# Graph attention on one Trainium2 core: the sixth chunk's four place products are issued ahead of its four transposing passes

## The reference, cut to what matters

```python
def gatv2_layer(x, Ws, bs, Wd, bd, attn, src, dst):
    hs = (x @ Ws + bs).reshape(N, H, HD)
    hd = (x @ Wd + bd).reshape(N, H, HD)
    hs_e = hs[src]
    e = jax.nn.leaky_relu(hs_e + hd[dst], SLOPE)
    logits = jnp.einsum('ehd,hd->eh', e, attn)
    m = jax.ops.segment_max(logits, dst, num_segments=N)
    ex = jnp.exp(logits - m[dst])
    s = jax.ops.segment_sum(ex, dst, num_segments=N)
    alpha = ex / s[dst]
    out = jax.ops.segment_sum(alpha[..., None] * hs_e, dst, num_segments=N)
    return jax.nn.elu(out).reshape(N, DM)
```

## Time and profile before

| what | value |
|---|---|
| median of three runs | 2142.82 us |
| the profiled execution | 2140.68 us, span 2138.9 us |
| granted TensorE clock, mean | 0.986 of 2.4 GHz |
| TensorE busy | 2052.9 us, 96% |
| VectorE busy | 1641.7 us, 77% |
| ScalarE busy | 1160.9 us, 54% |
| GpSimd busy | 975.4 us, 46% |
| passes of line 601 | 4368 instructions |
| products of line 605 | 4368 instructions |

### The profile page before, as it was taken

How to read it: one execution, slowest core, us unless ns; L and a number is a source line. 1 busy time by engine, 2 the same in 40 slices (tenths; PEclk the granted TensorE clock), 3 DMA queues, 4 the chain that set the end, 5 groups by cost and what they waited for, 6 DMA issues and landing times. The chain is left out here.

```text
span 2138.9 us, 85423 instructions
## 1 busy us (share of the span) xinstructions
PE 2052.9 (96%) x29551; PEld 1665.6 (78%) x29552; DVE 1641.7 (77%) x3719; ACT 1160.9 (54%) x3113; POOL 975.4 (46%) x1023
## 2 busy tenths in 40 slices
PE   7999999998999999999998899899999999999798
PEld 4665555555899999999997555599999999999676
DVE  5545883554799999999998764499999999999883
ACT  2101210014677777777775413477777777777583
POOL 0000010110677777777772311277777777777020
PEclk9999999999999999999999999999999999999899
DMA  6000233683888888888884224488888888888511
GB/s 202 1 0 16 74 105 121 185 208 78 248 270 269 274 270 270 271 268 272 270 273 136 87 91 128 131 264 272 269 270 272 271 263 275 271 266 275 185 49 51
DMA packets 184668, 415.48 MB, mean 194 GB/s; under 512 B 59967, under 2 KB 122693, under 8 KB 184557
## 3 DMA queue, kind: packets, MB, share of 16 engines
q0 software_dynamic: 59584, 298.64, 45.0%
q1 hardware_dynamic: 105899, 98.97, 14.9%
q10 hardware_dynamic: 19104, 16.79, 2.8%
HBM read 379.72 MB, written 23.13 MB: 188 GB/s over the span
## 5 line engine op out<-in xcount | busy, mean ns | idle before, releaser
L531 ACT ACTIVATE at_relu<-at_turned,ah_attn_size 128x512 f32<-128x512 f32 x1092 | 713.9, 688 | 306.4 <-PE at_turned L605 286.6
L507 POOL DMA_INDIRECT at_rows<-table,ah_index x360 | 425.2, 1181 | 175.9 <-POOL ah_index L495 71.7
L507 POOL DMA_INDIRECT ah_room<-table,ah_index x352 | 422.8, 1201 | 164.7 <-POOL ah_index L495 65.7
L711 DVE SCALAR_TENSOR_TENSOR at_relu<-at_relu,ah_pair_sign 128x512 f32<-128x512 f32 x546 | 376.8, 744 | 8.2 <-ACT at_relu L531 8.2
L741 DVE SCALAR_TENSOR_TENSOR sums<-sums,at_factor,at_total 128x97 f32 x1456 | 358.8, 308 | 5.4 <-PE at_total L647 2.2
L601 PE MATMUL at_turned<-ident,ah_room 128*128 128x128 f32 x2208 | 341.1, 277 | 19.3 <-PEq L1702 19.0
L601 PE MATMUL at_turned<-ident,at_rows 128*128 128x128 f32 x2160 | 331.0, 276 | 0.1
L601 PEld LDWEIGHTS at_turned<-ident,ah_room 128*128 128x128 f32 x2208 | 243.3, 142 | 40.5 <-issue 40.3
L601 PEld LDWEIGHTS at_turned<-ident,at_rows 128*128 128x128 f32 x2160 | 236.3, 141 | 19.9 <-issue 19.9
L731 DVE TENSOR_TENSOR at_spread<-at_lined,at_weight 128x1024 f32<-128x1024 bf16 x182 | 221.5, 1217 | 2.8 <-ACT at_weight L542 2.8
L605 PE MATMUL at_turned<-ah_place,dst_rows 96*128 96x128 bf16 x2208 | 215.7, 219 | 0.0
(11 more groups left out here) (315 smaller groups left out, 2884.7 us busy)
## 6 DMA issues: line engine op xcount, KB each, us to landing
at_flags<-run_flags SPq DMA_DIRECT2D x182, 64.0 KB
dst_rows<-pr_parts SPq DMA_DIRECT2D x76, 144.0 KB, 2.7
ah_place<-places SPq DMA_DIRECT2D x92, 96.0 KB
at_place<-places SPq DMA_DIRECT2D x90, 96.0 KB
table<-ah_room SPq DMA_DIRECT2D x20, 400.0 KB, 3.2
ah_room<-table,ah_index POOLq DMA_INDIRECT x368
at_lined<-lines SPq DMA_DIRECT2D x182, 32.0 KB
at_rows<-table,ah_index POOLq DMA_INDIRECT x360
```

The source lines that it names most:

```text
L507: pool.indirect_dma_start(rows[b][:, j, :], None, table, bass.IndirectOffsetOnAxis(index[b][:, j:j + 1], 0)).then_inc(gathered[b], 16)
L531: act.activation(relu[c][:], turned[chunk(b, c)][:], ACT.Relu, scale=attn_size[:, c:c + 1]).then_inc(bent, 1)
L711: dve.scalar_tensor_tensor(relu[c][:], relu[from_][:], pair_sign[:, c:c + 1], relu[c][:], ALU.mult, ALU.add).then_inc(joined, 1)
```

## The change

Inside `turn_chunk` the two loops become two functions, and for the sixth chunk (`c == KC - 1`) they are called in the other order. The first instruction of the chunk, now a product, has `start=True`; the last, now a pass, has `stop=True` and raises `turned_done`. The first five chunks are as before.

```diff
-                    for j in range(G):
-                        pe.matmul(into[j], rows[b][:, j, c * P:(c + 1) * P], ident[:], is_transpose=True, start=j == 0, stop=False)
-                    if c == 0:
-                        pe.wait_ge(local_loaded[b], place_there)
-                    for j in range(G):
-                        last = pe.matmul(into[j], dst_rows[0:SP_ROWS, bass.ds(at[j], 1), c * P:(c + 1) * P].rearrange("p o d -> p (o d)"),
-                                         place[b][:, j * P:(j + 1) * P], start=False, stop=j == G - 1)
-                    last.then_inc(turned_done, 1)
+                    def passes(first):
+                        for j in range(G):
+                            last = pe.matmul(into[j], rows[b][:, j, c * P:(c + 1) * P], ident[:], is_transpose=True,
+                                             start=first and j == 0, stop=not first and j == G - 1)
+                        return last
+
+                    def products(first):
+                        for j in range(G):
+                            last = pe.matmul(into[j], dst_rows[0:SP_ROWS, bass.ds(at[j], 1), c * P:(c + 1) * P].rearrange("p o d -> p (o d)"),
+                                             place[b][:, j * P:(j + 1) * P], start=first and j == 0, stop=not first and j == G - 1)
+                        return last
+
+                    if c == KC - 1:
+                        products(True)
+                        passes(False).then_inc(turned_done, 1)
+                    else:
+                        passes(True)
+                        if c == 0:
+                            pe.wait_ge(local_loaded[b], place_there)
+                        products(False).then_inc(turned_done, 1)
```

## The result

| | before | changed |
|---|---|---|
| median of 20 runs each | 2142.19 us | 2146.26 us |
| lowest to highest | 2140.58 to 2144.72 | 2143.72 to 2150.24 |
| profiled execution | 2140.68 us | 2143.72 us |
| its span | 2138.9 us | 2141.9 us |
| granted clock, mean | 0.986 | 0.985 |

The ratio is 1.0019, with an interval of 1.0012 to 1.0025. So the changed kernel is slower by 4.07 us, and the interval allows 2.6 to 5.4 us. The forecast was 2.8 us more, 2145.6 us, in a range from 2138.0 to 2152.

The account below looks back on a forecast made before the run. TensorE's matmul starts were taken to bound the kernel. Terms of 0.75 us (94 groups), 1.85 (44 first slots) and 0.2 (44 last slots) gave +2.8 on 2142.8, so 2145.6 us, range 2138.0 to 2152.

Parts of the forecast that it names:

- The bound: TensorE in the loop: no other engine holds it up, so time between two matmul starts is paid in full.
- The head: Sixth chunk's start, linear pass to first product: 0.14 us as before, gain 0, at most 0.03.
- rival C: Sixth chunk's start gains its 0.03 us; whole change -0.5 us, 2142.3, no change; chance 0.16.
- The middle: Sixth chunk's products 0.17 us, 0.055 to the first pass, three pass steps 0.33; gain of 0.055 where kinds meet.
- Rival D: Adding in place makes the sixth chunk's passes slow: pitch up a tenth, 0.044 per group, +8 us; chance 0.04.
- The tail: Sixth chunk's last pass to the messages' strips: 0.20 us instead of 0.15 behind a product, a loss of 0.055.
- Rival A: A pass ahead of strips costs what a product does, 0.15 us; sum -4.8 us, 2138.0; chance 0.12.
- The sequencer: Sixth chunk's last product needs 0.10 us lead behind its address instruction; late by 0.034 in first slots, middle slots on time.
- Rival B: Sixth chunk's last product needs more lead than 0.10 us; 2147.3 to 2158 us, likely about 2149; chance 0.16.
- The branch's cover: Loop's last slots: products late by 0.05 us hide behind the branch's wait, 0.698 within 0.703; cover 5 ns thick.
- The bank's wait and ScalarE: Sixth chunk's bank wait is met 1.2 us early and costs nothing; ScalarE stays 0.10 us early at the heads.
- The order of the two kinds as such is neutral: Sixth chunk: what is won where passes and products meet is given back at the strips; +8 ns per group.

Follow-up runs that it names:

- the fixed block in the old order: Kernel before, with the sixth chunk's products always reading block 0 of the target table, so without address instructions: 2139.74 against 2142.73 us, ratio 0.9986.
- the fixed block in the new one: Changed kernel, with the sixth chunk's products always reading block 0, so without address instructions: 2141.09 us, ratio 0.9994.
- the early load: Kernel before, with the next group's block numbers loaded behind the third chunk instead of between fourth and fifth: 2138.74 against 2143.35 us, ratio 0.9982.
- the split version: Changed kernel, with the sixth chunk as two products, four passes, two products: 2144.02 us, ratio 1.0007.
- the version with the fifth chunk too: Changed kernel, with products ahead of passes in the fifth chunk as well as the sixth: 2155.7 us, ratio 1.0061.
- the last two versions: Block 0 always read in fifth and sixth chunks: kernel before, 2138.18 us; changed kernel with only the fifth chunk products first, 2130.03 us.

## Why the prediction was right, point by point

- **The bound.** Starts of TensorE set the time: with the fixed block in the old order, the fixed block in the new one and the early load, the loops of the traces are 4.1, 3.1 and 4.6 us shorter than before, and the medians of the time 3.0, 1.6 and 4.6, each known to about 2 us.
- **The head.** 0.143 from linear pass to product, as taken. The 0.03 of rival C didn't come.
- **The middle.** 0.170 and 0.055 where the sequencer is on time; three steps of passes 0.333. Rival D has fallen: passes that add in place keep their 0.11.
- **The tail.** 0.202 behind a pass, with rows from another stage as the only ground; 0.147 behind a product in the split version. Rival A has fallen. The sentence of the Trainium skill cited in the prediction ("TensorEngine Tiling (Array Packing)", Tiling Modes, Key Properties) agrees, and gives no size.
- **The sequencer.** The need was taken as 0.10 from one starved example, and it is 0.101 to 0.103 in 88 slots here and in all 176 slots of the version with the fifth chunk too. The three kinds of slot came out at +42, +8 and +6 ns in the medians of their periods, against 42, 8 and 5. Rival B has fallen. Inside the 42 two small terms were wrong and cancelled. The 0.005 for the wait isn't there: the first address instruction of the sixth chunk takes 46 ns in all slots of the changed kernel. In its place, the first pass starts 0.064 behind a late product and not 0.055, which the sum had not. The lead in the middle slots is 0.171, forecast 0.16.
- **The branch's cover.** It held, barely: address instruction to message 0.704 before and 0.711 after, as medians. Without the branch it would be 0.102 + 0.064 + 0.334 + 0.202 = 0.702, so of the 5 ns of cover 2 were left.
- **The bank's wait and ScalarE.** In the first slot shown above, the sixth chunk's four address instructions start 0.124 us apart from 883.302 on, and ScalarE's second emptying had ended at 882.075, so the bank's wait cost nothing there. The heads' ninth matmul starts 110 to 174 ns after ScalarE's end (medians of the kinds of slot), more than the 53 at which it is held, so this is no wait in the changed kernel.

The terms sum to 2.8 us, the medians of the slots to 2.8 as well, and the slots one by one to 2.4, in loops that are 1.8 us longer. The time's median moved by 4.07. A cost of 2.8 is inside the interval (2.6 to 5.4), 2.4 is just below it, and outside the loops the profiled executions of all versions scatter by 3 us and more (943.8 to 946.9 us, once 951.3). Whether anything real is in the missing 1.3 to 1.7 us stays open: the changed kernel's 20 runs spread wider (6.5 us against 4.1), its profiled execution is the lowest of them, and one trace can't show what the longer ones have. That the forecast of 2145.6 us comes within 0.7 of the measured 2146.26 is in part luck: it starts from a median of three runs, 2142.82, that is 0.6 above the median of twenty.

One sentence of the prediction was too wide: "The order of the two kinds as such is neutral". It is neutral where strips follow. Where the drop follows, products first win 0.055 a group, as the last two versions show; that a pass hides the load of the drop's weights is the reason argued for, and it wasn't tested by itself. The misses of the experiments came from there, from taking the load of the block numbers as free for instructions that use no register, and from a pause of the sequencer that the late slots don't have.

**The best version.** With the early load and the fifth chunk products first, alone or with the sixth, 2136.2 to 2136.5 us were measured, ratios 0.9969 to 0.9974: 6 to 7 us under the kernel before, with the whole computation, and by adding the change's 4.1 some 10 to 11 under the changed one. Some 4.6 of that come from the load's place.

## What to carry to other kernels

When every matmul counts, read the distance from start to start, and price each neighbourhood (this kind ahead of that kind, strips, a small matmul) by a row of the same pair, from any stage. Count the sequencer's instructions as a queue of their own: a matmul whose operand's place comes from a register cost it 0.124 us here and needed 0.10 us of lead. Where the sequencer is short, matmuls that are slow and have fixed places belong ahead of such ones. Moving a register load to an earlier place helps only where the sequencer pauses in between; where it works without a break, taking instructions away is what is left, which wasn't tried here. Once TensorE is shortened, look what is late next; here ScalarE's cover of 0.05 us was used up by one reorder.

## What the runs showed of the hardware

- A four-byte matmul of 8 columns is two instructions, 84 ns apart behind a bf16 product and 31 ns behind a four-byte pass. That a long pass hides the load of the weights is the likely reason, and it wasn't measured by itself.
- From whole matmuls to strips it costs 0.092 to 0.093 us beyond the pitch of the last matmul, behind either kind (0.055 + 0.092, 0.109 + 0.093).
- A load of block numbers into registers delays also matmuls that use none: 0.34 instead of 0.23 us from the first product to the next pass, in the slots with the shorter lead, when it stands behind the first chunk.
- The lead that a product needs behind its address instruction is the same in every starved slot of two kernels, 101 to 103 ns.
